# A decoder's recurrence stage: one exponential of a sum of logarithms in place of root, gate and inverse decay, on pairs of batches

## The reference

```python
h = _rmsnorm(x, pre_norm_w)
a = jax.nn.sigmoid(h @ w_a + decay_bias)
i_gate = jax.nn.sigmoid(h @ w_i)
v = h @ w_v
input_signal = jnp.sqrt(jnp.clip(1.0 - a * a, 1e-08)) * (i_gate * v)
rec_out = _chunked_scan(a, input_signal)
x = x + rec_out @ out_proj_w
h2 = _rmsnorm(x, ffn_norm_w)
gate, up = jnp.split(h2 @ w_gate_up, 2, axis=-1)
return x + jax.nn.silu(gate) * up @ w_down
```

```python
cum_decay = jnp.exp(jnp.cumsum(jnp.log(jnp.clip(dc, 1e-10)), axis=2))
intra = cum_decay * jnp.cumsum(vc / jnp.clip(cum_decay, 1e-10), axis=2)
chunk_states = ic + cd * state[:, None, :]
return (chunk_states[:, -1], chunk_states)
```

## Time and profile before

| | |
|---|---|
| median of 3 runs | 1841.32 us (1838.14 to 1845.16) |
| profiled execution | 1833.95 us, its span 1832.3 us |
| TensorE busy | 1491.5 us, 81% of the span |
| VectorE busy | 1174.0 us, 64% |
| ScalarE busy | 826.3 us, 45% |
| POOL busy | 785.7 us, 43% |
| mean granted TensorE clock | 0.845 of full |

### The profile page before, as it was taken

The page is one execution under the profiler, slowest core; times in us unless marked ns, Lnnn a source line. Parts: engine busy times, 40 slices in busy tenths (PEclk is TensorE's granted clock), DMA queues, the critical chain, the costliest instruction groups (busy, mean ns, idle before and its releaser), DMA issues. The chain is left out here.

```text
span 1832.3 us, 27101 instructions
## 1 busy us (share of the span) xinstructions
PE 1491.5 (81%) x8788; PEld 1106.3 (60%) x8788; DVE 1174.0 (64%) x2993; ACT 826.3 (45%) x2146; POOL 785.7 (43%) x1207
## 2 busy tenths in 40 slices
PE   4899997799999949999883894055777779969999
PEld 3576774588888613333663683024555469957888
DVE  3587775355555769888354526986977769972222
ACT  2244442143444458888216213446666558842111
POOL 3488871166555557666221203555555422220000
PEclk8799996899999955555897897567988979978999
DMA  5100002000000045555400000020000030000000
GB/s 213 56 7 7 2 1 85 24 13 7 7 1 1 1 87 101 89 91 88 175 1 0 1 1 26 0 98 1 1 1 1 1 139 2 2 1 1 7 6 12
DMA packets 98379, 62.21 MB, mean 34 GB/s; under 512 B 88896, under 2 KB 93376, under 8 KB 96448
## 3 DMA queue, kind: packets, MB, share of 16 engines
q1 hardware_dynamic: 98240, 60.48, 12.3%
HBM read 38.44 MB, written 1.05 MB: 22 GB/s over the span
## 5 line engine op out<-in xcount | busy, mean ns | idle before, releaser
L101 PE MATMUL banks<-normed_t,arena_a 128*128 128x256 f32 x1104 | 256.8, 389 | 3.5 <-PEq L3203 3.5
L101 PEld LDWEIGHTS banks<-normed_t,arena_a 128*128 128x128 f32 x1104 | 215.1, 196 | 35.1 <-issue 4.4
L446 POOL TENSOR_TENSOR lut_weights<-lut_weights,arena_b 128x536 f32<-128x536 f32 x128 | 179.1, 1399 | 121.2 <-DVE arena_b L436 111.4
L605 POOL TENSOR_SCALAR work<-work,small 128x256 f32<-128x256 f32 (+1 forms) x384 | 176.5, 477 | 81.5 <-DVE small L597 81.3
L101 PE MATMUL banks<-arena_a 64*128 64x512 bf16 (+1 forms) x384 | 161.6, 540 | 30.9 <-PEq L3203 18.7
L1615 ACT ACTIVATE arena_a<-banks,work 128x1024 uint8<-128x1024 f32 x128 | 154.1, 1204 | 47.1 <-DVE work L1553 40.5
L1551 DVE TENSOR_REDUCE work<-banks 128x1 f32<-128x1024 f32 x128 | 155.4, 1214 | 24.2 <-PE banks L101 24.2
L1645 POOL TENSOR_SCALAR arena_a<-arena_a 128x1024 bf16<-128x1024 uint8 x128 | 132.1, 1045 | 64.6 <-DMA arena_a<-arena_a 62.5
L107 PE MATMUL banks<-identity,work 128*128 128x128 f32 x968 | 135.0, 281 | 20.0 <-ACT work L550 8.5
L585 ACT ACTIVATE work<-banks,small 128x256 f32<-128x256 f32 (+1 forms) x258 | 115.3, 458 | 62.4 <-DVE small L572 58.9
L107 PEld LDWEIGHTS banks<-identity,work 128*128 128x128 f32 x968 | 114.6, 147 | 34.6 <-POOL work L605 13.5
(11 more groups left out here) (411 smaller groups left out, 3440.6 us busy)
## 6 DMA issues: line engine op xcount, KB each, us to landing
arena_a<-in_L3f_wg SPq DMA_DIRECT2D x1, 4096.0 KB, 13.1
arena_b<-in_lut_idx SPq DMA_DIRECT2D x8, 268.0 KB, 3.3
arena_b<-in_L_wqn SPq DMA_DIRECT2D x1, 2048.0 KB, 12.4
arena_b<-in_L_wo SPq DMA_DIRECT2D x1, 2048.0 KB, 17.6
arena_a<-in_L_wq SPq DMA_DIRECT2D x1, 2048.0 KB, 7.5
arena_a<-in_L_wo SPq DMA_DIRECT2D x1, 2048.0 KB, 13.1
arena_a<-arena_a SPq DMA_TRANSPOSE x128, 2.5
arena_b<-in_L2f_gv SPq DMA_DIRECT2D x1, 2048.0 KB, 8.1
```

What stands on the lines that cost most here:

```text
L101: ins = t.matmul(out, lhs_t, rhs, start=start and i == 0, stop=stop and i == n - 1)
L446: g.tensor_tensor(o, o, lut_t[j % 2], ALU.add).then_inc(*summed.up(c * LUT + j))
L605: ins = g.tensor_scalar(e[:, c], e[:, c], A.rl[n % 2][:, 2 * hh + i:2 * hh + i + 1], 0.0, ALU.mult, ALU.add)
```

## The change

The algebra changes. With za = exp(-(a's projection + bias)) and zi likewise for i, the logarithms are ln(1 + za) = -ln a, ln(1 + zi) = -ln i, and ln(za (za + 2)) = ln(1 - a a) - 2 ln a. So the root, the input gate and the inverse of the summed decay are added up as logarithms and exponentiated at once ("factor"), and only multiplied by v. POOL clips za; VectorE forms za (za + 2) in one operation (`roots`) and the sum in a scan and three operations on two tensors (`exponents`). ScalarE scales the argument of the logarithm by 2^-20 and puts this back as the bias of the exponential. The carried state is added to the sum inside the chunk and then multiplied by the decay in one operation for each half of the features, so the product with the decay is left only for the first chunk.

The order changes too. Batches go in pairs (0, 1) and (2, 3) through ScalarE; TensorE makes the a projections of a pair, then the i projections, and all v projections last; batches 0 and 1 have made their states before VectorE comes to the exponents of 2 and 3; the scaling of batch b follows two steps behind its states, and its transposes stand ahead of the output product of batch b + 2. Those transposes now go to banks 4 to 7 instead of 6 and 7. The transposes of batch 1 are written twice. Batch 3's are placed after the second group of the feed-forward part. POOL adds to the residual in four pieces after the last scaling, each waited for only where it is read (`evacuate`).

```diff
@@ -1817,15 +1817,18 @@
+    def rec_bank(part, b):
+        return banks[4 + b] if part == "ffn" else banks[6 + b % 2]
     def rec_turn_scalar(part, b):
         a.wait_ge(*(yield turned, REC, part, b))
-        a.copy(*copied_t(b, banks[6 + b % 2].f)).then_inc(*xt_a.up(REC, part, b))
+        a.copy(*copied_t(b, rec_bank(part, b).f)).then_inc(*xt_a.up(REC, part, b))
     def rec_turn_tensor(part, b, empty=None):
         t.wait_ge(*(yield vs, REC, part, b))
         if empty:
             t.wait_ge(*(yield empty))
-        token_turns(banks[6 + b % 2].f, rec_hn[:, b * CB:(b + 1) * CB], id_f).then_inc(*turned.up(REC, part, b))
+        token_turns(rec_bank(part, b).f, rec_hn[:, b * CB:(b + 1) * CB], id_f).then_inc(*turned.up(REC, part, b))
@@ -1923,11 +1926,19 @@
-        buf = [[c.take(1024), c.take(512), c.take(512), big_b[:, 2048 + 512 * i:2560 + 512 * i]] for i in range(NB)]
+        buf = [[c.take(512), c.take(512), c.take(512), c.take(512), big_b[:, 2048 + 512 * i:2560 + 512 * i]] for i in range(NB)]
...
+        SMALL = 2.0 ** -20
+        unscaled = tiny[:, 72:73]
+        PAIRS = [(0, 1), (2, 3)]
+        a_bank, i_bank, v_bank = [0, 1, 4, 5], [2, 3, 0, 1], [2, 3, 4, 5]
@@ -1938,32 +1949,39 @@
+        def projected(j, b, bank):
+            for k2 in range(KH):
+                ins = products(t, bank.f[:, k2 * S:(k2 + 1) * S],
+                               [(W["wa6"][:, j * 512 + k * D + k2 * P:j * 512 + k * D + (k2 + 1) * P], of_batch(b, k)) for k in range(KH)])
+            ins.then_inc(*ts.up(s, "aiv", b, j))
         def tensor():
             def later(q):
-                if q == 0:
-                    for b in (2, 3):
-                        yield from rec_turn_tensor("ffn", b, (xt_a, s, "ffn", b - 2))
+                if q < 2:
+                    yield from rec_turn_tensor("ffn", 2 + q)
+                if q == 1:
+                    t.wait_ge(*(yield xt_a, s, "ffn", 1))
...
+            for pair in PAIRS:
+                for b in pair:
+                    t.wait_ge(*(yield xt_a, s, "rec", b))
+                    projected(0, b, banks[a_bank[b]])
+                if pair == PAIRS[0]:
+                    yield from rec_turn_tensor("rec", 3, (xt_a, s, "rec", 1))
+                for b in pair:
+                    if b >= 2:
+                        t.wait_ge(*(yield as_, s, "z", 0, b - 2))
+                    projected(1, b, banks[i_bank[b]])
             for b in range(NB):
-                if b == 1:
...
+                t.wait_ge(*(yield as_, s, "z", 1 - b // 2, b))
+                projected(2, b, banks[v_bank[b]])
             for b in range(NB):
+                if b >= 2:
+                    yield from rec_turn_tensor("ffn", b - 2)
                 t.wait_ge(*(yield vs, s, "states", b))
-                t.wait_ge(*(yield vs, s, "iv", 2 + b % 2))
                 if b >= 2:
                     t.wait_ge(*(yield vs, s, "x1", b - 2))
@@ -1971,15 +1989,61 @@
                 ins.then_inc(*ts.up(s, "out", b))
-            for b in range(2):
-                yield from rec_turn_tensor("ffn", b, (vs, s, "x1", b + 2))
+            yield from rec_turn_tensor("ffn", 1)
             yield from gated_tensor(F, later)
             yield MEET
         def vector():
             def evacuate(b):
+                v.wait_ge(*(yield gs, s, "x", b))
                 finish(s, b, banks[6 + b % 2].f)
-                yield from ()
+            def roots(b):
+                z, _, u_, _, _ = buf[b]
+                v.wait_ge(*(yield gs, s, "clip", b))
+                v.scalar_tensor_tensor(u_, z, 2.0, z, ALU.add, ALU.mult).then_inc(*vs.up(s, "u", b))
+            def exponents(b):
+                _, i_, u_, t_, cl = buf[b]
+                v.wait_ge(*(yield as_, s, "ln", b))
+                v.tensor_tensor_scan(cl, mask01, t_, 0.0, ALU.mult, ALU.add).then_inc(*vs.up(s, "sums", b))
+                v.wait_ge(*(yield as_, s, "ln_u", b))
+                v.scalar_tensor_tensor(u_, u_, 0.5, t_, ALU.mult, ALU.subtract).then_inc(*vs.up())
+                v.wait_ge(*(yield as_, s, "ln_i", b))
+                v.wait_ge(*vs.now())
+                v.scalar_tensor_tensor(t_, cl, CLIP, i_, ALU.min, ALU.subtract).then_inc(*vs.up())
+                v.wait_ge(*vs.now())
+                v.scalar_tensor_tensor(u_, u_, 0.5 * math.log(1e-8 * SMALL), t_, ALU.max, ALU.add).then_inc(*vs.up(s, "exponent", b))
+            def states_of(b):
+                cd, ci, u_, _, _ = buf[b]
+                st = states[:, b * 512:(b + 1) * 512]
+                v.wait_ge(*(yield as_, s, "factor", b))
+                v.wait_ge(*(yield ts, s, "aiv", b, 2))
+                v.tensor_tensor(ci, u_, banks[v_bank[b]].f, ALU.mult).then_inc(*vs.up())
+                v.wait_ge(*vs.now())
+                v.tensor_tensor_scan(u_, mask01, ci, 0.0, ALU.mult, ALU.add).then_inc(*vs.up())
+                s3, c3, u3 = (r.rearrange("p (k t) -> p k t", k=KH) for r in (st, cd, u_))
+                v.wait_ge(*vs.now())
+                v.tensor_tensor(s3[:, :, 0:CHUNK], u3[:, :, 0:CHUNK], c3[:, :, 0:CHUNK], ALU.mult).then_inc(*vs.up())
+                for lo in range(CHUNK, S, CHUNK):
+                    v.wait_ge(*vs.now())
+                    for k in range(KH):
+                        c_ = slice(k * S + lo, k * S + lo + CHUNK)
+                        v.scalar_tensor_tensor(st[:, c_], u_[:, c_], st[:, k * S + lo - 1:k * S + lo], cd[:, c_], ALU.add, ALU.mult).then_inc(*vs.up())
+                vs.all(s, "states", b)
+            def added_to_normed(b):
+                xs = nf[:, b * CB:(b + 1) * CB]
+                v.wait_ge(*(yield ts, s, "out", b))
+                v.tensor_tensor(xs, banks[6 + b % 2].f, xs, ALU.add).then_inc(*vs.up(s, "x1", b))
+            def scaled(b):
+                v.wait_ge(*(yield gs, s, "r2", b))
+                v.wait_ge(*vs.now())
+                rec_scaled_vector("ffn", b, r2, W["fn6"])
@@ -1991,58 +2055,24 @@
             yield from rec_vector(3)
-            for b in range(NB):
...
+            v.wait_ge(*(yield gs, s, "mask"))
+            for b in PAIRS[0]:
+                yield from roots(b)
+            for b in PAIRS[0]:
+                yield from exponents(b)
+            for b in PAIRS[1]:
+                yield from roots(b)
+            v.wait_ge(*(yield turned, s, "rec", NB - 1))
+            for n in range(NB + 2):
+                if n == 2:
+                    for b in PAIRS[1]:
+                        yield from exponents(b)
                 if n < NB:
-                    b = n
...
+                    yield from states_of(n)
+                if 0 <= n - 1 < NB:
+                    yield from added_to_normed(n - 1)
+                if 0 <= n - 2 < NB:
+                    yield from scaled(n - 2)
             yield from gated_vector(F, evacuate, later)
             yield MEET
@@ -2055,67 +2085,69 @@
-            for b in range(NB):
...
+            for n in range(len(PAIRS) + 1):
+                if n < len(PAIRS):
+                    for b in PAIRS[n]:
+                        z = buf[b][0]
+                        a.wait_ge(*(yield ts, s, "aiv", b, 0))
+                        for k2 in range(KH):
+                            c_ = slice(k2 * S, (k2 + 1) * S)
+                            ins = a.activation(z[:, c_], banks[a_bank[b]].f[:, c_], ACT.Exp, scale=-1.0, bias=ndb[:, k2:k2 + 1])
+                        ins.then_inc(*as_.up(s, "z", 0, b))
+                    if n == 0:
+                        yield from rec_turn_scalar("rec", 3)
+                    for b in PAIRS[n]:
+                        a.wait_ge(*(yield ts, s, "aiv", b, 1))
+                        a.activation(buf[b][1], banks[i_bank[b]].f, ACT.Exp, scale=-1.0).then_inc(*as_.up(s, "z", 1, b))
+                if n:
+                    for b in PAIRS[n - 1]:
+                        z, _, u_, _, cl = buf[b]
+                        a.wait_ge(*(yield vs, s, "sums", b))
+                        a.activation(z, cl, ACT.Exp, scale=-1.0).then_inc(*as_.up())
+                        a.wait_ge(*(yield gs, s, "mask"))
+                        a.wait_ge(*(yield vs, s, "exponent", b))
+                        a.activation(u_, u_, ACT.Exp, bias=unscaled).then_inc(*as_.up(s, "factor", b))
+                if n < len(PAIRS):
                     a.wait_ge(*as_.now())
-                a.activation(z, z, ACT.Ln, bias=1.0).then_inc(*as_.up(s, "ln", b))
...
+                    for b in PAIRS[n]:
+                        z, _, u_, t_, _ = buf[b]
+                        a.wait_ge(*(yield vs, s, "u", b))
+                        a.activation(t_, z, ACT.Ln, bias=1.0).then_inc(*as_.up(s, "ln", b))
+                        a.activation(u_, u_, ACT.Ln, scale=SMALL).then_inc(*as_.up(s, "ln_u", b))
+                    for b in PAIRS[n]:
+                        i_ = buf[b][1]
+                        a.activation(i_, i_, ACT.Ln, bias=1.0).then_inc(*as_.up(s, "ln_i", b))
+            for b in range(NB + 2):
+                if b < NB:
```

(14 more changed lines are left out.)

108 lines of the change are left out of this document (4 added, 104 removed).

## The result

The changed kernel took 1812.3 us (median of 4 runs, 1811.54 to 1816.27) beside 1839.87 us for the kernel before (4 runs, 1838.14 to 1845.16): ratio 0.985, 95% interval 0.9824 to 0.9876. That is 27.6 us by the medians where 22.8 were forecast. The two profiled executions differ less: spans of 1832.3 and 1811.1 us, 21.2 us.

A forecast was written before the change was run, and what follows sets the result against it. The recurrence's four-leg chain before TensorE's first feed-forward matmul was taken as the limit; that matmul moves from 1029.1 to 1006.3, 22.8 us, so 1841.3 becomes 1818.5 us, range 1810 to 1831.

The forecast's parts named there:

- The sum: First feed-forward matmul at 1006.3 instead of 1029.1 us, 22.8 us earlier; whole kernel 1818.5 us.
- What bounds the stage: Feed-forward part bound by TensorE, recurrence not; the first feed-forward matmul's start counts, and nothing behind it gets shorter.
- Leg (a): Projections and first exponentials on TensorE and ScalarE: with pairs, the Ln table loads near 967 instead of 979.0 us.
- Leg (b): Logarithms to exponents on ScalarE and VectorE: first state product at 977.2 instead of 1004.1 us, 26.9 us earlier.
- Leg (c): VectorE's states: 3.56 instead of 4.74 us a batch; with exponents, sums and scaling 24.7 us, to 1001.9.
- leg (d): From batch 1's scaling to the first feed-forward matmul: transposes with handover 0.7, last output product 2.9, repeated transposes 0.5 us.
- dearer or cheaper operations: Rival, chance 0.12: VectorE's new operations at upper bounds gain 13.0 us (1828.3), at lower bounds 28.8 (1812.5).
- Batch 0's squares: They wait behind ScalarE's last Exp; inverse root ready at 995.7, scaling due 995.95: just covered, otherwise up to 0.5 us.
- Stalled start: Rival, chance 0.10: Silu or POOL's residual pieces hold the feed-forward start, costing 2 to 4 us; 1822 us.
- Slower by the clock: Rival, chance 0.03: TensorE's clock stays low in the feed-forward part; 1862.5 us with half of some 400 instructions at the lower level.

The follow-up runs named there:

- Output products first: Changed kernel with the transposes of batches 0 and 1 behind the output products of 2 and 3, and batch 1's transposes written once: 1807.29 us.
- v last: Kernel before with one thing of the change, all a projections, then all i projections, and the v projections last: 1830.63 us.
- algebra: Kernel before with the new root, exponents and factor; projection order, carries, scaling as before; POOL's four pieces and transposes of batches 2, 3 as changed: 1827.22 us.
- one table before: Kernel before with the one table set for exp and ln loaded by name ahead of the stage: 1841.79 us.
- old carry: Changed kernel with the carries as before, a 512-column product with the decay and two 128-column operations per chunk: 1819.05 us.

## Why the prediction was right

Its steps, counted from the first projection:

- **The sum**: 23.2 us at G for 22.8. That the whole time stayed in the range is partly luck: 1812.3 is 6.2 us below the forecast of 1818.5, and close to the 1812.5 that the prediction gave for cheaper operations of VectorE, though these cost what was forecast. The 6.2 are 1.7 in the feed-forward part, 0.4 at G, and 4.1 from outside the stage, 1.5 of them the new median of the kernel before (1839.87 for 1841.3).
- **What bounds the stage**: right. The gain at G went through to the end; nothing behind E changed by more than 0.8 us.
- **Leg (a)**: the first Ln load was forecast at 11.0 and came at 10.5; in four kernels that are the same up to there it came between 10.5 and 11.2.
- **Leg (b)**: the first state product was forecast at 21.1 and came at 20.8. An operation on two tensors with a number took 0.66 to 0.69, as taken from the row of the plain product. Two of the exponents' operations took 0.91 and 0.98 (above), at the time when POOL's two clips took 1.90 where one takes 0.61 alone. The second half of ScalarE's chain was covered: its Ln did not wait for VectorE, and VectorE did not wait for it. With the chunks of leg (c) inside their bounds too, this settles the rival of dearer or cheaper operations.
- **Leg (c)**: this is the step that missed, both in a size and in the path. An operation of 64 columns was put at 0.23 and a chunk at 0.42; measured were 1.51 for three chunks, 0.50 each, so the batch took 3.73 for 3.56. And the sum had no wait for TensorE in it. It knew that the last output product stands behind batch 1's transposes and these behind batch 1's scaling, but not that batch 0's transposes do the same to the product of batch 2: they wait for batch 0's scaling, the product stands behind them, and VectorE's sum of batch 2 waits 0.89 us for it, ahead of batch 1's scaling. So from the first state product to the end of that scaling it was 26.2 us for 24.7 (0.7 from the batches, 0.9 from the wait). The point from which leg (d) counts came at 47.1 for 45.8. "Output products first" shows the price of the order of TensorE's queue: about 2.6 us.
- **Leg (d)**: 4.4 us forecast, 2.7 measured. The last product ran at the higher level, 1.7 us to the next instruction, where 2.9 was taken as a mean, and transposes and handover cost 0.9 for 1.2. (The terms that the prediction names for this leg add up to 4.1, not 4.4.) That the errors of legs (c) and (d) cancel to 0.4 is luck.
- **Batch 0's squares** waited for ScalarE's last Exp, as said: they start at 996.78, and the scaling at 1000.49 follows the sum without a wait. Covered.
- **Stalled start**: it did not happen. The third group of feed-forward matmuls is followed by the fourth without a pause (48 in one run from 1018.17), Silu began 9.9 us after G (10.1 forecast), and POOL's four pieces took 4.94 us (timeline of POOL):

```profile
1013.97 4.94 POOL L2150 TENSOR_TENSOR residual<-residual,big_a 128x512 f32<-128x512 f32 x4 [0.99 <-DVE big_a L1810]
```

- **Slower by the clock**: the opposite came. The granted clock of the feed-forward part was 0.98 where it was 0.97 before, and its first 16 matmuls were 1.8 us shorter. The forecast had them unchanged, and this is the term that makes 24.9 of 23.2.
- **The clock as a taker** of small gains was in no rival. In four of the experiments (v last, algebra, one table before, old carry) the last output product took 1.4 to 1.6 us more than in the kernel that was edited.

## What to carry to other kernels

When a chain of four batches passes through two engines, split it so that the engine that ends it (VectorE here) starts on the first batches while the other still works on the last; the gain at the end (6.95) is roughly that of the first start (14.0) less the work that now lies in between (6.5). On an in-order queue put the work that someone waits for ahead of work that is only needed later: a group of transposes ahead of each of two output products cost about 2.6 us, because the transposes themselves had to wait. And measure an edit by a landmark that is counted from the start of its own stage, since the entry into this one moved by 7.5 us between executions. Then look where between the landmarks the difference arose: of the 2.8 us that one table seemed to gain, 1.0 was the entry.
